# The states' product of a Mamba-style block, split into high and low parts: three reduced-precision products in place of one full float32 product

## The reference

```python
# b=2 batches, nc=4 chunks of 128 tokens, 128 heads of 64 channels, 8 groups, N=128 states
xch = (hs * dt[..., None]).reshape(b, nc, CHUNK, H, P)
decay_states = jnp.exp(A_cum[..., -1:] - A_cum)
states = jnp.einsum('bzlhn,bhzl,bzlhp->bzhpn', Bc, decay_states, xch)
...
new_states = jnp.einsum('bhzc,bchpn->bzhpn', decay_chunk, states_p)
prev = new_states[:, :-1]
Y_off = jnp.einsum('bzlhn,bzhpn,bhzl->bzlhp', Cc, prev, jnp.exp(A_cum))
```

## Time and profile before

| what | value |
|---|---|
| device time, median of 3 runs | 1635.05 us (1633.94 to 1636.73) |
| the profiled execution, own time | 1639.27 us |
| its span, first to last instruction | 1637.5 us |
| PE busy | 1598.2 us (98%), 9616 matmul records |
| PE weight loads busy | 1357.8 us (83%) |
| VectorE busy | 1261.2 us (77%) |
| ScalarE busy | 1147.9 us (70%) |
| GpSimd busy | 711.3 us (43%) |
| mean granted TensorE clock | 0.991 of full |

### The profile page before, as it was taken

How to read it: one execution, slowest core, us unless ns; L and a number is a source line. 1 busy time by engine, 2 the same in 40 slices (tenths; PEclk the granted TensorE clock), 3 DMA queues, 4 the chain that set the end, 5 groups by cost and what they waited for, 6 DMA issues and landing times.

```text
span 1637.5 us, 26761 instructions
## 1 busy us (share of the span) xinstructions
PE 1598.2 (98%) x9616; PEld 1357.8 (83%) x9616; DVE 1261.2 (77%) x1974; ACT 1147.9 (70%) x2002; POOL 711.3 (43%) x543
## 2 busy tenths in 40 slices
PE   7799999999999999999999999999999999999997
PEld 4678888888888888888888888888888888888876
DVE  6577777887778787787778877787877877787776
ACT  5398668776777767876787766777678767777741
POOL 1145445354443543454453544435444444434542
PEclk9799999999999999999999999999999999999999
DMA  5533233323232332332333232233223323233211
GB/s 200 186 111 106 78 110 99 102 84 120 87 97 95 110 97 85 114 103 77 111 98 103 84 120 88 86 106 110 90 92 114 102 77 112 93 108 94 75 43 52
DMA packets 88244, 164.56 MB, mean 100 GB/s; under 512 B 23344, under 2 KB 39728, under 8 KB 87856
## 3 DMA queue, kind: packets, MB, share of 16 engines
q1 hardware_dynamic: 88112, 162.85, 30.5%
HBM read 157.03 MB, written 5.77 MB: 99 GB/s over the span
## 4 chain that ended last, share of the span: by engine, by line
PE 90%; issue 2%; DVE 2%; POOL 1%; ACT 1%; DVEq 0%; POOLq 0%; ACTq 0%
PE g_bank L714 9%; PE g_bank L715 8%; PE g_bank L716 8%; PE d_bank L733 7%; PE x_bank L714 7%; PE x_bank L715 7%; PE x_bank L716 7%; PE d_bank L773 3%; PE d_bank L775 3%; PE d_bank L774 3%; PE x_bank L773 3%; PE x_bank L774 3%; PE x_bank L775 3%; PE state_bank L722 2%; PE state_bank L740 2%; PE turn_bank L740 2%
## 5 line engine op out<-in xcount | busy, mean ns | idle before, releaser
L1294 POOL TENSOR_TENSOR w_low<-raw,w_high 128x512 fp32r<-128x512 f32 x141 | 182.3, 1293 | 580.2 <-ACT w_high L915 580.2
L1068 DVE SCALAR_TENSOR_TENSOR hs<-x_bank,cols,hs 128x1022 f32<-128x1022 f32 (+2 forms) x192 | 245.4, 1278 | 98.5 <-ACT hs L935 96.2
L925 ACT ACTIVATE scores<-scores,tables 128x128 f32<-128x128 f32 x1024 | 312.4, 392 | 0.0
L1308 POOL TENSOR_TENSOR y<-y,gate 128x512 f32<-128x512 f32 x128 | 188.7, 1494 | 205.5 <-DVE y L1130 205.5
L935 ACT ACTIVATE hs<-x_bank,cols 128x1024 f32<-128x1024 f32 x64 | 77.0, 1203 | 278.3 <-PE x_bank L716 278.3
L714 PE MATMUL g_bank<-x_high,w_high 128*128 128x512 f32 x624 | 251.2, 403 | 1.3 <-DVE bc L1147 1.3
L715 PE MATMUL g_bank<-x_low,w_high 128*128 128x512 f32 x624 | 244.0, 391 | 0.0
L716 PE MATMUL g_bank<-x_high,w_low 128*128 128x512 f32 x624 | 243.7, 391 | 0.0
L714 PE MATMUL x_bank<-x_high,w_high 128*128 128x512 f32 x512 | 199.6, 390 | 0.5 <-PEq L146 0.5
L716 PE MATMUL x_bank<-x_high,w_low 128*128 128x512 f32 x512 | 199.2, 389 | 0.0
L715 PE MATMUL x_bank<-x_low,w_high 128*128 128x512 f32 x512 | 199.2, 389 | 0.0
(11 more groups left out here) (185 smaller groups left out, 3492.2 us busy)
## 6 DMA issues: line engine op xcount, KB each, us to landing
scores<-sums_dram SPq DMA_DIRECT2D x128, 512.0 KB, 4.9
raw<-w_in SPq DMA_DIRECT2D x144, 256.0 KB, 2.9
grown_rows<-grown_dram SPq DMA_DIRECT2D x256, 96.0 KB, 2.8
out_raw<-w_out SPq DMA_DIRECT2D x64, 256.0 KB, 3.5
xt<-x SPq DMA_DIRECT2D x8, 256.0 KB, 5.6
mixed<-x SPq DMA_DIRECT2D x1, 2048.0 KB, 12.2
out<-mixed SPq DMA_DIRECT2D x8, 256.0 KB, 2.0
table_dram<-table SPq DMA_DIRECT2D x2, 768.0 KB, 3.2
```

The lines of the kernel that those rows point to most:

```text
L925: op = s.activation(at, at, ACT.Relu, bias=col[:, r, c:c + 1], scale=-1.0)
L1068: v.scalar_tensor_tensor(out=hs[:, q % 2, :, i:], in0=x_bank[:, :, 0:SEQ - i], scalar=cols[:, q, TAPS - 1 - i:TAPS - i], in1=hs[:, q % 2, ...
L1294: pool.tensor_tensor(w_low[:, slot], raw[:, slot], w_high[:, slot].bitcast(F32), ALU.subtract)\
L1308: pool.tensor_tensor(y[:, b], y[:, b], gate[:, q % 2, b], ALU.mult).then_inc(y_ready, 1)
```

## The change

B of the group is kept in two parts: ScalarE writes b_high (fp32r) where it wrote b_tok, and VectorE subtracts to make b_low. xdecay is split for each unit and batch in the same way: ScalarE makes xdecay_high, in its program after `finish` of the unit before and ahead of the high part of the output weights; VectorE makes xdecay_low, after `scores` (and after b_low, in the first unit of a group) and ahead of `y_low_part`. The states' product becomes three fp32r matmuls for each chunk, and waits for xdecay_low in place of xdecay. To make room, the scratch kept for dynamically built DMAs is halved; the kernel's 715 DMAs are all issued by SP, and none is added or moved.

```diff
-DMA_SCRATCH = 8192
+DMA_SCRATCH = 4096
...
-        b_tok = sb("b_tok", [P, BATCH, LATER, STATE])
+        b_high, b_low = (sb(n, [P, BATCH, LATER, STATE], F32R) for n in ("b_high", "b_low"))
+        xdecay_high = sb("xdecay_high", [P, BATCH, LATER, PAIR, HEAD_DIM], F32R)
+        xdecay_low = sb("xdecay_low", [P, BATCH, LATER, PAIR, HEAD_DIM], F32R)
...
             def states(k, b):
-                pe.wait_ge(xdecay_ready, BATCH * k + b + 1)
+                pe.wait_ge(xdecay_low_ready, BATCH * k + b + 1)
+                flat = lambda t, c: t[:, b, c].rearrange("p r d -> p (r d)")
                 for c in range(LATER):
-                    mm = pe.matmul(head_bank[b][:, c * P:(c + 1) * P], b_tok[:, b, c],
-                                   xdecay[:, b, c].rearrange("p r d -> p (r d)"), start=True, stop=True)
+                    to = head_bank[b][:, c * P:(c + 1) * P]
+                    pe.matmul(to, b_high[:, b, c], flat(xdecay_high, c), start=True, stop=False)
+                    pe.matmul(to, b_high[:, b, c], flat(xdecay_low, c), start=False, stop=False)
+                    mm = pe.matmul(to, b_low[:, b, c], flat(xdecay_high, c), start=False, stop=True)
                 mm.then_inc(states_added, 1)
...
@@ ScalarE @@
-                s.activation(b_tok[:].rearrange("p b c n -> p b (c n)"), turned_b[:, :, 0:LATER * P], ACT.Copy)\
-                 .then_inc(b_tok_ready, 1)
+                s.activation(b_high[:].rearrange("p b c n -> p b (c n)"), turned_b[:, :, 0:LATER * P], ACT.Copy)\
+                 .then_inc(b_high_ready, 1)
+
+            def split_xdecay(k, b):
+                s.wait_ge(xdecay_ready, BATCH * k + b + 1)
+                s.activation(xdecay_high[:, b].rearrange("p c r d -> p (c r d)"),
+                             xdecay[:, b].rearrange("p c r d -> p (c r d)"), ACT.Copy).then_inc(xdecay_high_ready, 1)
...
                     if now:
+                        for b in range(BATCH):
+                            split_xdecay(k, b)
...
@@ VectorE @@
+            def xdecay_low_part(k, b):
+                v.wait_ge(xdecay_high_ready, BATCH * k + b + 1)
+                v.tensor_tensor(xdecay_low[:, b], xdecay[:, b], xdecay_high[:, b].bitcast(F32), ALU.subtract)\
+                 .then_inc(xdecay_low_ready, 1)
+
+            def b_low_part(g, turned_b):
+                v.wait_ge(b_high_ready, g + 1)
+                v.tensor_tensor(b_low[:].rearrange("p b c n -> p b (c n)"), turned_b[:, :, 0:LATER * P],
+                                b_high[:].rearrange("p b c n -> p b (c n)").bitcast(F32), ALU.subtract)\
+                 .then_inc(b_low_ready, 1)
...
                     if j == UNITS - 1 and not last:
                         keep_bc(g + 1)
+                    if j == 0:
+                        b_low_part(g, g_bank if g > 0 else d_bank)
+                    for b in range(BATCH):
+                        xdecay_low_part(k, b)
                     if prev:
                         y_low_part(prev[1], prev[2])
```

More of the change, by code:

```diff
@@ L582, in mixer @@
          conv_ready) = (sem(n) for n in names)
-        (bc_silu, b_turned, b_tok_ready, bc_product, bc_ready, c_ready, var_done, std_ready, rstd_ready, out_done,
+        (bc_silu, b_turned, b_high_ready, b_low_ready, xdecay_high_ready, xdecay_low_ready, bc_product, bc_ready, c_ready, var_done, std_ready, rstd_ready, out_done,
          added, mixed_ready) = (
-            sem(n) for n in ("bc_silu", "b_turned", "b_tok_ready", "bc_product", "bc_ready", "c_ready", "var_done",
+            sem(n) for n in ("bc_silu", "b_turned", "b_high_ready", "b_low_ready", "xdecay_high_ready", "xdecay_low_ready", "bc_product", "bc_ready", "c_ready", "var_done",
                              "std_ready", "rstd_ready", "out_done", "added", "mixed_ready"))
@@ L727, in diagonal @@
                 if k == 0:
-                    pe.wait_ge(b_tok_ready, 1)
+                    pe.wait_ge(b_low_ready, 1)
                 pe.wait_ge(scores_ready, BATCH * k + b + 1)
@@ L828, in body @@
                         if j == 0:
-                            pe.wait_ge(b_tok_ready, g + 1)
+                            pe.wait_ge(b_low_ready, g + 1)
                         for b in range(BATCH):
```

## The result

| | before | after |
|---|---|---|
| median, fastest to slowest of 4 runs | 1635.89 us (1633.94 to 1637.21) | 1692.8 us (1690.54 to 1694.54) |
| profiled execution, own time / span | 1639.27 / 1637.5 us | 1693.11 / 1691.4 us |
| mean granted clock | 0.991 | 0.986 |

The kernel is slower: ratio 1.0348 (1.0335 to 1.0361), 56.9 us between the medians. The time lies inside the range given, 10.8 us above the value given.

The account below looks back on a forecast made before the run. TensorE was taken as the bound. Terms 42.8 + 3.6 + 1 + 0.5 - 1 = +46.9 us on the profiled 1639.27 gave 1686.2, or 1682 us against the median; 8 in 10 range 1669 to 1703 us.

Parts of the forecast that it names:

- a pair at the load's price: States' product on TensorE: 384 more pairs of weight load and matmul at 0.1115 us each, +42.8 us.
- The splits cost nothing in the middle: Middle units: the added VectorE and ScalarE work is done before TensorE needs it, at no cost.
- The tightest cover: Last unit of a group, with the mask: first low part ends 0.5 us before TensorE comes for it.
- The first units: Units 0 to 2: TensorE waits for low parts behind `scores`; +3.6 us in unit 0, 1 us in units 1 and 2.
- The last unit: Unit 63: states wait for VectorE's late scores, partly covered; +0.5 us, bounds 0 and 1.5.
- the cover of about 1 us: Last unit: some delay is hidden, since VectorE finishes y and its sums began a microsecond later anyway.
- starting waits: Start of the kernel: part of the starting waits goes, -1 us.
- Rival A: States' product: moving columns alone set a pair, 0.057 us, so faster, median 1619 us; chance 0.07.
- C: States' product: fp32r loads overlap more, 0.084 us a pair, 1650 us; chance 0.04.
- B: States' product: narrow fp32r products take 0.223 or 0.227 us each, median 1810 to 1815 us; chance 0.09.
- D: TensorE waits for low parts in all 64 units, a third of a microsecond each, 21 us, median 1703; chance 0.05.

Follow-up runs that it names:

- half_weights3: reduced3 with 64 weight columns in place of 128, so half the state is left out; 1619.77 us, 0.9901 of the kernel before.
- wide3: reduced3 with 256 moving columns in place of 128, neighbouring chunks overwriting each other; 1687.44 us, 1.0317 of the kernel before.
- reduced1: Kernel before with the states' operands written as fp32r, one product for each chunk, no splits or low parts; 1597.62 us, ratio 0.976.
- reduced3: Kernel before with fp32r operands and the same product added three times for each chunk, no splits or low parts; 1674.14 us, ratio 1.0234.
- plain_with_splits: Changed kernel with all splits and waits, but the states' product plain float32 from b_high and xdecay; 1648.34 us, 1.0068 of the kernel before.
- start_early: Changed kernel with unit 0's low parts made ahead of `scores`, its high parts between the batches' decays; 1686.68 us, 1.031 of the kernel before.
- end_early: Changed kernel with the low parts of units 62 and 63 made ahead of `scores`; 1689.28 us, 1.0324 of the kernel before.
- bf16_split: Changed kernel with early splits in units 0, 62 and 63 and all four parts in bfloat16; 1621.74 us, 0.9909 of the kernel before.
- bf16_3: reduced3 with the two operands in bfloat16 in place of fp32r; 1617.1 us, 0.9888 of the kernel before.

## Why the prediction was right, and where it was off

- **TensorE as the bound, and a pair at the load's price: right.** Starts 0.11 us apart, loads of 196 ns, and half_weights3 and wide3 say that the load sets them. The term was 42.8 us and measured 39.9 (64 blocks of 0.624). Mis-sized was the block, 2.10 forecast and 2.05 found: six pairs more are 0.67 us, but the block gave 0.05 back at its start. The second fp32r matmul starts 0.06 us after the first (896.51 and 896.57 above; reduced1 and reduced3 alike), the second plain one 0.11; behind the last one it is 0.21 us to the next product in both.
- **The splits cost nothing in the middle: right.** 1420.32 us in after and in reduced3, which has no splits and the full DMA scratch; 1384.17 in before and in plain_with_splits, which has them all. The tightest cover, unit 31, was put at 0.5 us; in after the two subtractions start there at 847.71 and the states at 848.75, so 0.5 us it was.
- **The first units: the mechanism right, the size wrong.** The terms were 3.6 us for unit 0 and 1 for units 1 and 2, and 11.7 were measured for the three. The wait in unit 0, some 5 us in the forecast, is 5.25. Left out was TensorE's clock behind it: at the lower level the states lose 4.00 - 2.05 = 1.95 us, `diagonal` 3.61 - 1.90 = 1.71, the gate projection 6.16 - 5.58 = 0.58. In units 1 and 2 `diagonal` takes 3.36 and 3.45 us in place of 1.90, 3.0 together. That is 7.2 of the 11.7; the other 4.5 are the waits, near the 4.6 forecast. start_early shows the link for unit 0: without the wait the clock stays up and the block is short.
- **The last unit: wrong.** The term was +0.5 and measured +5.9. The states came at 1623.33 in after, behind 5.95 us of idling, and ran with `diagonal` at the lower clock: 4.03 + 3.61 in place of the 2.1 + 1.9 reckoned, 3.6 us of the 5.4 missed. Some 0.9 us more came before unit 63's `scores`, 0.58 of it a wait of TensorE in unit 62. The rest is the cover of about 1 us that I claimed from VectorE's sums, and it was not there: from the start of unit 63's `carry` to the end takes 60.44 us before (from 1577.08) and 60.42 after (from 1630.97), so whatever made `carry` late made the end late. The rows could have warned of the clock. In rows 18 the first six matmuls of `carry` last 1.65 us, where six of them last 0.83 in unit 33; the granted clock of before was down there already, behind two idle gaps of 1.99 and 1.11 us in its `diagonal`:

```profile
1577.00:1583.00 6.00, 5.92 (x24) 5.31 (x25) 5.01 (x12) 0.00 (x0) 1.85 (x2) 0.67 0.01 1
```

  end_early's order takes back all of the 5.9.
- **The starting waits and the median.** The profiled execution of before lay 3.4 us above its later median, that of after 0.3 above its own. The forecast took 4.2 off for both, which made the value lower than it needed to be: the difference is 53.8 us between the profiled ones, 56.9 between the medians. The -1 for starting waits rested on no row, and the -3.7 found in its place goes with the prologue's clock, not with the change. So there is luck in the value: 7.1 and 5.4 us too little at the two ends, less 2.9 too much for the pairs and less 2.7 that the prologue's clock gave, are the 6.9 us between 1686.2 and 1693.11.
- **Rival A** (moving columns alone) and **C** (0.084 us a pair) fell with starts of 0.111 us. For an operand in bfloat16 A's price is the true one: 0.056 us against the 0.057 that it was given. It was wrong of the type, not of the engine. **B** (0.22 us a pair) fell with reduced3: 38.5 us, not 171 or more. **D** (waits in every unit) fell with the two equal middles.
- **What stays open.** Why the clock holds behind a wait of 1.3 us when plain or bfloat16 products follow, and falls when narrow fp32r ones do. Two differences go together there, the type and how long the block lasts (1.43, 1.11 and 2.05 us), and no run parts them. The number of matmuls alone is not it: bf16_split has the same eighteen.

The chances were 0.9 for slower, and it is; the forecast's own bounds, 1674 to 1693, just held 1692.8.

## What to carry to other kernels

Before a float32 product is split into reduced ones, measure the distance of starts of its pairs and count the loads: with 128 moving columns on 128 columns of four-byte weights the load is the price, two pairs become three, and the split loses. The same split in bfloat16 halves the price of a pair, and won 0.9% here, if its bits suffice. Where the engine goes from wait to wait, compare a block's length with the same block elsewhere: twice the length shows the lower clock before anything is run. And where a change puts a wait of several microseconds ahead of TensorE, add to it the work behind it at half the clock (4.2 us behind the 5.25 of unit 0); there the order of a few small instructions on another engine was worth 11.7 us, at no cost to the middle.

## What the runs showed of the hardware that I had not expected

- **A load's price depends on the type.** 128 x 128 weights: record 192 ns and pair 0.111 us in fp32r (reduced3), record 98 ns and pair 0.056 us in bfloat16 (bf16_3). The Trainium skill, "TensorE: Matmul & The Clock Gate", section "Weight-path perf modes — Fast Weight Load (FWL) and DoubleRow", has a fast load come on by itself when there are 128 weights and the type is not FP32; the trace agrees for bfloat16, and fp32r behaves as FP32 does. The rule weighed in the prediction, a load of columns over 1.2 GHz (the same page of the Trainium skill, section "LDWEIGHTS (loading the stationary operand)"), by estimate 107 ns for 128 columns, comes near the 0.111 us of the four-byte types here, but not the 0.056 us of bfloat16.
- **The clock falls behind a wait, and the fall costs more than half of what the wait did, on top of it.** In unit 0, 5.25 us of waiting were followed by 8 us at a granted clock of 0.50, which lost 4.2 us; in unit 63, 5.95 us of waiting by a loss of 3.6. The same page of the Trainium skill, section "What's actually happening", has the array at 1.2 GHz once it has been idle; the trace agrees with that for unit 0 and unit 63. Units 1 and 2, with 1.34 and 1.36 us of waiting and 0.55 and 0.53 behind them, are cases that the waiting alone does not explain.
- **256 moving columns cost hardly more than 128**, 0.119 us a pair against 0.111 in fp32r. Half of the 0.227 of a 512-column pair is 0.114, so at 256 the two sides of a pair are nearly even.
